# A graph attention layer: one-hots and slot addresses made one period earlier, the slot gather issued behind the K|V gathers

## The reference, cut to what matters

```python
for l in range(L):                      # L = 2, H = 8 heads of DH = 64
    q = ((x @ Wq[l].T + bq[l]) * scaling).reshape(n, H, DH)
    k = (x @ Wk[l].T).reshape(n, H, DH)
    v = (x @ Wv[l].T).reshape(n, H, DH)
    scores = jnp.einsum('ehd,ehd->eh', q[tgt], k[srcidx])
    m = jax.ops.segment_max(scores, tgt, num_segments=n)
    p = jnp.exp(scores - m[tgt])
    s = jax.ops.segment_sum(p, tgt, num_segments=n)
    w = p / (s[tgt] + 1e-16)
    agg = jax.ops.segment_sum(w[:, :, None] * v[srcidx], tgt, num_segments=n)
    attn = agg.reshape(n, D) @ Wo[l].T + bo[l]
    x = _batchnorm(x + attn, g1[l], beta1[l])
    ...
```

## Time and profile before

| | |
|---|---|
| median of 3 runs | 3262.51 us |
| the profiled execution | 3271.22 us |
| its span | 3269.9 us |
| first attention, steady part | about 545 to 1345 us of the span |
| second attention | about 1840 to 2520 us of the span |
| PE, DVE, ACT, POOL busy over the span | 87%, 51%, 39%, 34% |

### The profile page before, as it was taken

How to read it: one execution, slowest core, us unless ns; L and a number is a source line. 1 busy time by engine, 2 the same in 40 slices (tenths; PEclk the granted TensorE clock), 3 DMA queues, 4 the chain that set the end, 5 groups by cost and what they waited for, 6 DMA issues and landing times.

```text
span 3269.9 us, 78219 instructions
## 1 busy us (share of the span) xinstructions
PE 2847.2 (87%) x32206; PEld 1996.0 (61%) x32206; DVE 1677.8 (51%) x3300; ACT 1270.2 (39%) x3609; POOL 1098.5 (34%) x1109
## 2 busy tenths in 40 slices
PE   6999997999989998677799799889886785899998
PEld 5877875666666666355488566666664462444444
DVE  5237774555454544535513355555555357555554
ACT  3324444455544544212332355555554112222221
POOL 0000004666666555200001477777773001111100
PEclk8999998999999999788899899999998897899999
DMA  6542007888888888521024699999996221011100
GB/s 210 221 153 89 30 30 249 296 306 303 299 295 296 292 290 280 147 68 59 30 98 150 218 353 351 345 351 353 347 347 203 62 85 39 26 39 39 48 32 15
DMA packets 223590, 608.82 MB, mean 186 GB/s; under 512 B 37008, under 2 KB 43792, under 8 KB 223219
## 3 DMA queue, kind: packets, MB, share of 16 engines
q0 software_dynamic: 137088, 466.78, 40.6%
q1 hardware_dynamic: 86131, 136.85, 12.5%
HBM read 525.96 MB, written 103.29 MB: 192 GB/s over the span
## 4 chain that ended last, share of the span: by engine, by line
PE 66%; DMA 16%; DVE 6%; issue 6%; POOL 4%; ACT 2%; SPq 1%; POOLq 0%; DVEq 0%; ACTq 0%
PE ps L1106 8%; DMA stage<-Qd,segs 7%; PE ps L2320 5%; PE ps L1129 5%; PE ps L2341 5%; PE ps L555 4%; DMA Y<-KVd,srcE 4%; PE ps L556 4%; PE ps L557 4%; PE ps L1141 3%; PE ps L915 3%; PE ps L620 2%; PE ps L622 2%; PE ps L621 2%; PE ps L1697 2%
## 5 line engine op out<-in xcount | busy, mean ns | idle before, releaser
L1026 POOL DMA_INDIRECT Y<-KVd,srcE x449 | 438.1, 976 | 146.2 <-issue 107.0
L1106 PE MATMUL ps<-ident,Y 128*128 128x128 f32 x1796 | 287.1, 283 | 38.0 <-DMA Y<-KVd,srcE 30.5
L1301 ACT ACTIVATE stage<-ps,stage 128x128 f32<-128x128 f32 x832 | 293.2, 372 | 22.5 <-DVE stage L1213 20.6
L1026 POOL DMA_INDIRECT WA<-KVd,srcE x186 | 182.0, 979 | 330.9 <-PE ps L557 267.0
L1282 ACT ACTIVATE G<-ps 128x512 f32<-128x512 f32 x315 | 188.7, 600 | 255.5 <-PE ps L1106 254.4
L1282 ACT ACTIVATE work<-ps 128x512 f32<-128x512 f32 x309 | 185.6, 601 | 241.5 <-PE ps L1106 239.6
L555 PE MATMUL ps<-Wh,xs 128*128 128x512 f32 x600 | 238.8, 398 | 38.0 <-DVE xs L495 38.0
L1106 PEld LDWEIGHTS ps<-ident,Y 128*128 128x128 f32 x1796 | 200.6, 142 | 112.5 <-issue 70.3
L1035 POOL DMA_INDIRECT stage<-Qd,segs x104 | 105.9, 1018 | 472.0 <-DVE G L1247 292.2
L556 PE MATMUL ps<-Wl,xs 128*128 128x512 f32 x600 | 236.7, 394 | 0.0
L557 PE MATMUL ps<-Wh,xs 128*128 128x512 f32 x600 | 236.7, 394 | 0.0
(11 more groups left out here) (337 smaller groups left out, 6471.4 us busy)
## 6 DMA issues: line engine op xcount, KB each, us to landing
KVd<-stage SPq DMA_DIRECT2D x96, 256.0 KB, 2.0
aggd<-work SPq DMA_DIRECT2D x6, 2048.0 KB, 7.4
Qd<-stage SPq DMA_DIRECT2D x48, 256.0 KB, 2.0
G<-aggd SPq DMA_DIRECT2D x48, 256.0 KB, 2.7
Y<-KVd,srcE POOLq DMA_INDIRECT x449
Y<-in_x SPq DMA_DIRECT2D x4, 1536.0 KB, 14.7
G<-mixq SPq DMA_DIRECT2D x24, 256.0 KB
mixd<-rowsb SPq DMA_DIRECT2D x24, 256.0 KB
```

What stands on the lines that cost most here:

```text
L1026: pool.indirect_dma_start(out=kvs[a], out_offset=None, in_=KVd[l][:, :], in_offset=bass.IndirectOffsetOnAxis(ap=srcE[:, n:n + 1], axis=0)) ...
L1106: mm = pe.transpose(bank[:, k * P:(k + 1) * P], kvs[a][:, k * P:(k + 1) * P], ident[:, :])
L1301: last = act.activation(pT[g % len(pT)][:, P * i:P * (i + 1)], SC[g % 2][:, P * i:P * (i + 1)], ACT.Exp, bias=smin[:, t:t + 1], scale=-1.0 ...
```

## The change

In the first attention (`l == 0`) three things move; the second attention keeps its order. TensorE's `turn_hot(b+2)` moves from the end of the odd period to behind the second tile of the even period of the same block. VectorE's `empty_hot(b+2)`, which ends in the slot addresses, moves with it from the end of the odd to the end of the even period, and `one_hot` runs one block further ahead to feed it. GpSimd's slot gather of an odd period moves from ahead of that period's four K|V gathers to behind them. The table of the PSUM banks is changed to the same order. No instruction is added or removed.

```diff
--- before.py
+++ after.py
@@ -971,10 +971,13 @@
             order += [("k", n) for n in range(LOOK[l])]
             for g in range(NQ + AGG_AT):
                 b = g // 2
-                order += [("k", n) for n in range(4 * g + LOOK[l], min(4 * g + LOOK[l] + 4, ET))]
+                for i in range(4):
+                    order += [("k", n) for n in (4 * g + LOOK[l] + i,) if n < ET]
+                    if l == 0 and g % 2 == 0 and i == 1 and b + 2 < NJ:
+                        order.append(("hot", b + 2))
                 if g % 2 == 0 and b + 1 < NJ:
                     order.append(("q", b + 1))
-                if g % 2 and b + 2 < NJ:
+                if l == 1 and g % 2 and b + 2 < NJ:
                     order.append(("hot", b + 2))
                 if 0 <= g - 1 < NQ:
                     order.append(("p", g - 1))
@@ -1060,14 +1063,16 @@
             at = KV
             for g in range(NQ + AGG_AT + 2):
                 j = (g + 3) // 2
-                if g % 2 and j < NJ:
+                if l == 1 and g % 2 and j < NJ:
                     fetch_slots(j)
-                j = (g - 2 - AGG_AT) // 2
-                if g % 2 == AGG_AT % 2 and 0 <= j < NJ:
-                    scatter(j)
+                x = (g - 2 - AGG_AT) // 2
+                if g % 2 == AGG_AT % 2 and 0 <= x < NJ:
+                    scatter(x)
                 while at < ET and (at - KV) // 4 <= g - AGG_AT:
                     fetch(at)
                     at += 1
+                if l == 0 and g % 2 and j < NJ:
+                    fetch_slots(j)
 
         def attend_pe(l, side):
             pe.wait_ge(q_out, NT * (l + 1))
@@ -1159,12 +1164,14 @@
                         turn_k(4 * g + LOOK[l] + i)
                     if g < NQ:
                         score(4 * g + i)
+                    if l == 0 and x == 0 and i == 1 and b + 2 < NJ:
+                        turn_hot(b + 2)
                     if i == 2 and g >= AGG_AT:
                         gather(g - AGG_AT)
                     next(side, None)
                 if x == 0 and b + 1 < NJ:
                     turn_q(b + 1)
-                if x == 1 and b + 2 < NJ:
+                if l == 1 and x == 1 and b + 2 < NJ:
                     turn_hot(b + 2)
                 if 0 <= g - 1 < NQ:
                     turn_p(g - 1)
@@ -1246,6 +1253,8 @@
                 dve.memset(qblk[i], 0.0)
                 last = dve.memset(probs[i], 0.0)
             last.then_inc(filled, 1)
+            if l == 0:
+                one_hot(2)
             for n in range(LOOK[l]):
                 if n % 4 == K_DVE[l]:
                     empty_k(n)
@@ -1259,15 +1268,17 @@
                 if 4 * g + LOOK[l] + 1 < ET:
                     empty_k(4 * g + LOOK[l] + 1)
                 next(side, None)
-                if x == 1 and b + 2 < NJ:
+                if l == 1 and x == 1 and b + 2 < NJ:
                     one_hot(b + 2)
+                if l == 0 and x == 1 and b + 3 < NJ:
+                    one_hot(b + 3)
                 if 0 <= g - 1 < NQ:
                     normalise(g - 1)
                 next(side, None)
                 if g >= AGG_AT and (g - AGG_AT) % 2:
                     empty_agg((g - AGG_AT) // 2)
                 next(side, None)
-                if x == 1 and b + 2 < NJ:
+                if x == l and b + 2 < NJ:
                     empty_hot(b + 2)
 
         def attend_act(l, side, begin, work_free):
```

## The result

The changed kernel takes 3371.7 us, the median of 4 runs (3364.03 to 3378.16), against 3266.9 us before (4 runs): 1.031 times as long, 95% interval 1.028 to 1.033, some 100 us more. The direction was forecast, the size was not: 3320 us with a range to 3352. The profiled execution took 3373.20 us, its span 3371.9, and the page says at once where to look: the chain of waits has the slot gather at 14% of the span where it had 7%.

What follows compares the result with a forecast made beforehand. TensorE was taken to bound the first attention; -48 us of K|V waits and +105 us of slot-gather waits gave +57 us on the 3262.5 us median, 3320 us, range 3256 to 3352 us.

Steps and rivals of the forecast that it cites:

- K|V waits gone, 48 us: First attention, TensorE: K|V gathers issued 3.85 us earlier in odd periods, so all 48.1 us of waits for them go.
- Slack from issue to need, 3.1 us: First attention: from GpSimd's issue of the slot gather, behind four K|V gathers, to turn_q on TensorE, 3.1 us.
- Landing behind four K|V gathers, 5.3 us: First attention: the slot gather takes 5.3 us from issue to arrival, between bounds of 3.95 and 5.96 us.
- the stall of 2.15 us: TensorE at turn_q, first attention: wait per block for the slot gather, 5.3 - 3.15 = 2.15 us.
- the 105 us: TensorE, first attention: total wait for slot gathers of blocks 3 to 51, 49 x 2.15 = 105 us.
- The sum of the waits, +57 us: Whole kernel: 48 us of K|V waits gone, 105 us of slot-gather waits added, +57 us.
- rival 4: First attention: slot gather lands in 6.8 us, stall 3.65 us, total +131 us, 3393 us; part of the 0.70 chance.
- The block of 17.4 us: First attention: a block of the changed kernel takes 17.4 instead of 16.3 us.
- Early one-hots and addresses cost nothing: VectorE and TensorE, first attention: same instructions one period earlier, done at 816.0 ahead of turn_q at 817.7; nothing is paid.
- Rival 3: First attention: slot gather lands under 3.1 us, no stall, -48 us, 3214 us; chance 0.08.
- The high end of the range, 3352 us: Slot gather landing of 5.96 us, stall 2.8 us, -48 + 138 = +90 us; about 0.1 chance above it.

Runs made afterwards that it cites:

- filled kernel: Changed kernel plus 16 throw-away identity transposes ahead of each turn_q of blocks 3 to 51, first attention: 3317.0 us, 1.014 of the kernel before.
- order alone: Kernel before with only the first attention's slot gather moved behind the four K|V gathers, one-hots and addresses late as before: 3371.6 us, ratio 1.032.
- behind three: Changed kernel, but the slot gather stands behind the third of its period's four K|V gathers: 3262.7 us, 0.998 of the kernel before.
- the first place: Kernel before with one-hots and addresses one period earlier, slot gather still ahead of the four K|V gathers: 3685.6 us slower chip, 3196.4 us faster chip.

## Why the prediction was right in direction and wrong in size

1. *K|V waits gone, 48 us.* Right: 0.7 us are left.
2. *Slack from issue to need, 3.1 us.* Nearly right: the median over 49 blocks, the way of each slot gather less TensorE's wait for it, is 3.3 us (3.54 us in the block shown).
3. *Landing behind four K|V gathers, 5.3 us.* A little low: the median of the 49 slot gathers in the chain of waits of the changed kernel is 5.67 us (4.27 to 6.74). Landing was 0.4 us and slack 0.2 us longer than I took, so the stall of 2.15 us came out at 2.3 us, and the 105 us at 112. In the two other profiles with this order the median landing is 5.5 and 5.3 us.
4. *The sum of the waits, +57 us.* Right as a sum of waits: TensorE's idle time grew by 52 us. The slot gather cost 7 us more than I took, and 15 us of TensorE's smaller waits went, which I had left alone (before, 45.9 of the 61.0 us of idle time in the stretch were K|V waits). That the sum came out within 5 us is in part luck, since the two misses go opposite ways.
5. *The step that failed* is the last sentence of rival 4: "A lower granted clock would go the same way; the windows show 0.99 and 1.00 with waits of both kinds, so I give it little." It was no rival but a second term of the forecast itself, +52 us, as large as the first. I read the clocks of 0.99 and 1.00 as showing that waits don't lower it, but the waits for data in those rows are 1.7 us at most in the first attention, and none of them is the 2.3 us stall that I was forecasting for every block. Nor was the clock of the kernel before untouched by waits. Its stretch has 5 falls and is 11 us busier than at full clock; one of them stands behind the wait in the first of these rows, and the second row gives the clock just after (TensorE's timeline, then a window):

```profile
1236.18 0.63 PE L1106 MATMUL ps<-ident,Y 128*128 128x128 f32 x4 [1.56 <-DMA Y<-KVd,srcE]
```

```profile
1237.00:1240.00 3.00, 3.00 (x73) 2.38 (x66) 0.00 (x0) 0.44 (x1) 2.09 (x4) 0.50 0.93 299
```

An average over 800 us hid them. The filled kernel shows the term by itself: the same late slot gather without the fall of the clock is 49 us faster. The block of 17.4 us that I forecast took 18.3.
6. *Early one-hots and addresses cost nothing.* Right: with the slot gather behind the K|V gathers, with or without them, the time is the same, and with it ahead TensorE is idle for 1.9 us.
7. *The rivals.* Rival 3 needed a landing under 3.1 us, and none in the first attention of the changed kernel was that short. The fit of the Trainium skill ("DMA: Bandwidth & Descriptors", section "Anatomy of one DMA — SWDGE (gpsimd) path"), an estimate of 2.6 us for this gather, is met by no row: the shortest there is 4.27 us. It describes one DMA, not one behind four. When the K|V gathers ahead landed the profile does not show, so what the slot gather waits for on its way is not shown either. The high end of the range, 3352 us, was built on the landing alone and so had no room for the clock.

On the row of 1.06 us against 0.60 us for the same four transposes bears the Trainium skill, "TensorE: Matmul & The Clock Gate", section "HAM oscillation — how this bites in real kernels", which describes a kernel whose DMA waits drop the array to half speed for the work that follows. The trace agrees in kind, with a granted clock of 0.50 behind the wait of 2.32 us; here waits shorter than those of that example were enough for some falls.

## What to carry to other kernels

Where one queue serves several consumers, price a move on it by the slack of what is moved: its issue, counted in the issues ahead of it, plus a landing taken from a loaded queue, against the moment of need. Two halves of one change can have opposite signs, and here the good half (addresses early, slot gather first) was worth -73 us while the order alone cost +101 us, and together they made +97 us. Where a change puts a new wait on TensorE in every block, like the 2.3 us here, add a second term for the clock behind it: here 39 to 63 us on 111 to 116 us of idle time, a third to a little over a half. With throw-away matmuls in the same wait the clock stayed at 1.00, and 49 us of the 170 us came back.

## What the runs showed that I had not expected

- The price of the clock goes with the number of its falls, not with the sum of the waits. Busy time over the 702.4 us of full clock: 11 us with 5 falls (before), 21 us with 9 (behind three), 39 us with 21 (order alone), 59 and 63 us with 32 and 33 (the changed kernel, two profiles): about 2 us for each. Not every wait of the same length has a fall behind it, and why one has and another has not, these runs do not show.
- TensorE can be brought to 702.4 of 704.3 us busy in this stage; there the DMA engines are at 0.93 and 325 GB/s, near the 0.97 of the earlier trace rows. So the first attention before the change was 70 us over its TensorE bound. That is more than the 48 us of K|V waits, and more than the 61 us of idle time in the stretch, since part of it was the clock.
- The same program took 3893 us in one set and 3270 us in the others, 19% apart, each set on another chip, and the order of four variants was another there: on the slower chip the slot gather behind two K|V gathers beat the first place by 101 us, on the faster ones it lost by 17 us. Whether it is the chip or something else of that set is not shown.
